# A three-layer field-interaction kernel: V and A as streaming matrix products, A reordered through a DRAM scratch, five replicas of X, one mixed 128-row tile

## The reference

```
Xi = X0                                    # [b, 32, d]
for W, b in ((W1, b1), (W2, b2), (W3, b3)):
    Wr = W.reshape(128, 32, m)             # m = fields of Xi: 32, then 128, 128
    Xi = einsum('bhd,bmd,ohm->bod', X0, Xi, Wr) + b[None, :, None]
    pools.append(Xi.sum(axis=-1))
y = concat(pools) @ fc_W.T + fc_b          # [64, 1]
```

## Time and profile before

| what | value |
|---|---|
| median of 3 runs | 107.69 us (107.32 to 108.24) |
| the profiled execution | 108.17 us, its span 106.4 us |
| around the span in the profiled execution | 1.77 us |
| PE busy | 81.1 us of the span |
| DVE, ACT, POOL busy | 62.7, 34.8, 38.5 us |
| moved by DMA | 15.64 MB |

### The profile page before, as it was taken

The page is one execution under the profiler, slowest core; times in us unless marked ns, Lnnn a source line. Parts: engine busy times, 40 slices in busy tenths (PEclk is TensorE's granted clock), DMA queues, the critical chain, the costliest instruction groups (busy, mean ns, idle before and its releaser), DMA issues.

```text
span 106.4 us, 960 instructions
## 1 busy us (share of the span) xinstructions
PE 81.1 (76%) x303; PEld 60.8 (57%) x303; DVE 62.7 (59%) x87; ACT 34.8 (33%) x66; POOL 38.5 (36%) x31
## 2 busy tenths in 40 slices
PE   0042692006999999934999999999999999999921
PEld 0031570004899879934767766776677666866710
DVE  0239999998600029959995999829987011020072
ACT  4008400019500277462809722076190200201100
POOL 2033099930700079955602309245062204022000
PEclk9999999755555555555589999999999999999998
DMA  3959999920599998971074643700000000000000
GB/s 94 402 135 353 419 431 419 434 117 0 112 110 125 393 404 250 116 310 65 0 219 176 194 200 89 305 3 0 0 6 0 0 0 0 0 0 0 0 0 0
DMA packets 3464, 15.64 MB, mean 147 GB/s; under 512 B 516, under 2 KB 644, under 8 KB 2180
## 3 DMA queue, kind: packets, MB, share of 16 engines
q1 hardware_dynamic: 3460, 15.59, 45.0%
HBM read 14.27 MB, written 0.00 MB: 134 GB/s over the span
## 4 chain that ended last, share of the span: by engine, by line
PE 69%; DVE 16%; DMA 5%; ACT 4%; issue 3%; SPq 0%; DVEq 0%
PE x_ps L538 27%; PE a_ps L538 27%; PE a_ps L599 11%; DMA rep<-xr 5%; DVE w_sb L180 5%; DVE v L476 2%; DVE z_ps L406 2%; ACT feat L313 2%; DVE feat L415 2%; DVE rows_sb L437 1%; PE a_ps L526 1%; ACT v_all L313 1%; ACT a_sb L313 1%; DVE total L509 1%; DVE total L506 1%
## 5 line engine op out<-in xcount | busy, mean ns | idle before, releaser
L538 PE MATMUL x_ps<-feat,w_hi 128*128 128x512 f32 x64 | 27.9, 495 | 2.4 <-DMA fc_all<-fc 2.4
L406 DVE TENSOR_TENSOR z_ps<-rep 128x512 f32<-128x512 f32 x24 | 21.2, 910 | 13.2 <-DMA rep<-xr 12.3
L538 PE MATMUL a_ps<-feat,a_hi 128*128 128x512 f32 x64 | 21.9, 403 | 0.0
L251 POOL TENSOR_TENSOR z_pool<-rep 128x512 f32<-128x512 f32 x8 | 14.9, 1858 | 15.3 <-DMA rep<-xr 13.6
L538 PEld LDWEIGHTS x_ps<-feat,w_hi 128*128 128x128 f32 x64 | 15.1, 236 | 7.0 <-DMA fc_all<-fc 2.8
L313 ACT ACTIVATE feat<-z_ps 128x512 fp32r<-128x512 f32 x24 | 13.9, 592 | 14.1 <-DVE z_ps L406 14.1
L285 POOL TENSOR_TENSOR x<-x 128x512 f32<-128x512 f32 x6 | 8.5, 1413 | 23.5 <-DVE x L466 23.5
L466 DVE SCALAR_TENSOR_TENSOR x<-a_ps,vec,x 128x512 f32<-128x512 f32 x8 | 6.0, 744 | 18.5 <-PE a_ps L538 18.5
L538 PE MATMUL x_ps<-feat,w_lo 128*128 128x512 f32 x32 | 15.6, 488 | 1.6 <-DVE w_tail L456 1.6
L415 DVE TENSOR_TENSOR feat<-z_ps,feat 128x512 fp32r<-128x512 f32 x24 | 16.0, 682 | 1.0 <-ACT feat L313 0.8
L599 PEld LDWEIGHTS a_ps<-v_all,w_sb 128*128 128x128 f32 x60 | 14.6, 331 | 1.6 <-issue 0.9
(11 more groups left out here) (66 smaller groups left out, 69.0 us busy)
## 6 DMA issues: line engine op xcount, KB each, us to landing
rep<-xr SPq DMA_DIRECT2D x8, 1024.0 KB, 5.4
w_sb<-w SPq DMA_DIRECT2D x4, 512.0 KB, 8.8
w_sb<-w SPq DMA_DIRECT2D x2, 1024.0 KB, 13.5
w_sb<-w SPq DMA_DIRECT2D x1, 560.0 KB, 3.8
tail<-z_hi SPq DMA_DIRECT2D x2, 256.0 KB, 5.4
xp<-x SPq DMA_DIRECT2D x1, 512.0 KB, 8.1
lin<-xp_lo SPq DMA_DIRECT2D x1, 512.0 KB, 6.7
xa<-x SPq DMA_DIRECT2D x1, 256.0 KB, 6.9
```

The source lines that it names most:

```text
L251: nc.gpsimd.tensor_tensor(z_pool[:, c % 2, :], rep[:, c % 2, left, :], rep[:, c % 2, right, :], ALU.mult).then_inc(zp_done, 1)
L406: nc.vector.tensor_tensor(z_ps[:, k, :], rep[:, c % 2, left, :], rep[:, c % 2, right, :], ALU.mult).then_inc(z_done, 1)
L538: last = nc.tensor.matmul(bank, w, f, **kw)
```

## The change

- V is a product on PE: `window` is zero but for the column of fc, and 32 matmuls (128 x 32 stationary, 128 columns of W3 streaming in f32) put the 32 fields of V on 32 rows in four column groups. One transpose brings it back. W3 is loaded in its own order, in pieces of 1 KB.
- A is 8 f32 matmuls with V stationary (64 columns) and 512 columns of W2 streaming. ACT saves them (`save_a`), six DMAs store them in a DRAM scratch `a_dram`, and eleven DMAs load them back in feature order, each pair in both orders, in pieces of 512 bytes. No transpose of A is left. DVE adds the two orders (`make_a`) inside chunk 3.
- W1 comes from the host in feature order, so its transposes go too.
- `rep` has five replicas instead of four, in two DMAs. The first holds the left fields of all pairs.
- The tail, and X in high and low parts, are one tile of 128 rows (`mixed`), filled by four DMAs of 16 rows and two of 32 rows from SBUF to SBUF. `lin_hi` goes.
- The order of PE, ACT and DVE is written out anew; the first reduction over d stands ahead of the last product.

```diff
-J = P // H
+J = 4
+REPS = TILES + 1
+X_HI, X_LO, Z_HI, Z_LO, Z_HI2, Z_PAD = 0, 32, 64, 80, 96, 112
+A_ROWS, A_COLS = 64, H + HALF
+ROW = A_COLS * M
+ROUNDS = 4
+    a_dram = nc.dram_tensor("a_dram", (A_ROWS, A_COLS * M), f32, kind="Internal").ap()
-        tail = sb("tail", [3 * HALF, CHUNKS, N], f32r)
-        lin = sb("lin", [3 * H, CHUNKS, N], f32r)
-        rep = sb("rep", [P, 2, 4, N])
+        mixed = sb("mixed", [P, CHUNKS, N], f32r)
+        rep = sb("rep", [P, 2, REPS, N])
...
 # sync
-                    sp.wait_ge(lin_hi_done, c - 1)
-                sp.dma_start(rep[:, c % 2, :, :], xr[c]).then_inc(rep_in[c % 2], 16)
+                sp.dma_start(rep[:, c % 2, 0:2, :], xr[c, :, 0:2, :]).then_inc(rep_in[c % 2][0], 16)
+                sp.dma_start(rep[:, c % 2, 2:, :], xr[c, :, 2:, :]).then_inc(rep_in[c % 2][1], 16)
+            def store_a(g, t, col):
+                to = bass.AP(a_dram.tensor, col * M, [[ROW, A_ROWS], [8 * M, 2], [1, N]])
+                sp.dma_start(to, at_sb[64 * g:64 * g + 64, t:t + 2, :]).then_inc(a_out, 16)
+            def load_f(to, offset, dims):
+                sp.dma_start(to, bass.AP(a_dram.tensor, offset, dims + [[1, M]])).then_inc(f_in, 16)
...
+            for t in range(ROUNDS):
+                part = slice(t * 8 * M, (t + 1) * 8 * M)
+                sp.dma_start(w2_sb[:, part], w2[:, part]).then_inc(w2_in[t], 16)
+            sp.dma_start(xp[:, :, :].rearrange("p d b -> p (d b)"),
+                         x.rearrange("h (c n) -> (h c) n", c=4)).then_inc(xp_in, 16)
+            for row, part, done in ((Z_HI, z16_hi, hi16_done), (Z_HI2, z16_hi, hi16_done),
+                                    (Z_PAD, z16_hi, hi16_done), (Z_LO, z16_lo, lo16_done)):
                 sp.wait_ge(done, 1)
+                sp.dma_start(mixed[row:row + HALF, :, :].bitcast(f32), part[:, :].bitcast(f32)).then_inc(z16_in, 16)
             load_replicas(2)
+            for row, part, done in ((X_HI, xp_hi, xp_hi_done), (X_LO, xp_lo, xp_lo_done)):
+                sp.wait_ge(done, 1)
+                sp.dma_start(mixed[row:row + H, :, :]..., part[:, :]...).then_inc(x_lin_in, 16)
             load_replicas(3)
-            sp.wait_ge(xp_lo_done, 1)
-            sp.dma_start(lin[2 * H:3 * H, :, :]..., xp_lo[:, :]...).then_inc(lin_lo_in, 16)
+            sp.wait_ge(a_saved, 2)
+            for g in range(2):
+                store_a(g, 0, 4 * g)
+                store_a(g, 0, H + 4 * g)
+            sp.wait_ge(a_saved, 4)
+            for g in range(2):
+                store_a(g, 2, HALF + 4 * g)
+            sp.wait_ge(zeros_done, 5)
+            sp.wait_ge(a_out, A_OUT)
+            for k in range(TILES):
+                load_f(f1[:, k, :], 4 * k * ROW, [[ROW + M, H], [ROW, J]])
+                load_f(f2[:, k, :], 4 * k * M, [[ROW + M, H], [M, J]])
+            load_f(f1[Z_HI:Z_PAD, TILES, :], HALF * ROW, [[0, 3], [ROW + M, HALF]])
+            load_f(f2[Z_HI:Z_PAD, TILES, :], HALF * M, [[0, 3], [ROW + M, HALF]])
+            load_f(f1[0:Z_HI, TILES, :], FC2_ROW * ROW, [[0, 2], [M, H]])
             for c in range(4, CHUNKS):
                 load_replicas(c)
...
 # scalar: hi(1, 3), xp_hi, q_sb, save_a(0), hi(2, 0), save_a(1), hi(2, 1), save_a(2), hi(2, 2),
 #   save_a(3), hi(2, 3), save_x1(0), save_x1(1), hi(3, 0..3), save_x1(2), a_hi, hi(4, 0..3), ...
+            def save_a(t):
+                act.wait_ge(a_ready, t + 1)
+                copy(at_sb[:, t, :], round_ps[t][:, :]).then_inc(a_saved, 1)
...
 # vector
+            def make_a():
+                dve.wait_ge(f_in, F_IN)
+                both_orders(f1, f2, f_sum)
+            for c in range(1, CHUNKS):
+                mult(c, 0)
+                mult(c, 1)
+                lo(c, 0)
+                mult(c, 2)
+                lo(c, 1)
+                if c == 3:
+                    make_a()
+                lo(c, 2)
+                lo(c, 3)
+                if c == 3:
+                    a_low()
+                if c >= 5:
+                    product(c - 5)
+            for c in range(3, CHUNKS - 1):
+                product(c)
             dve.wait_ge(acc_done, CHUNKS - 2)
             nc.vector.tensor_reduce(total[:, 0, :], ...)
+            product(CHUNKS - 1)
             dve.wait_ge(prod_done, CHUNKS)
             nc.vector.tensor_reduce(total[:, 1, :], ...)
...
 # tensor
+            x1_main(0)
+            pe.wait_ge(window_done, 1)
+            for i in range(8):
+                if i % 2 == 0:
+                    pe.wait_ge(w3_in[i // 2], 16)
+                for g in range(4):
+                    last = nc.tensor.matmul(vt_ps[32 * g:32 * g + 32, :], window[:, H - 1 - i:2 * H - 1 - i],
+                                            w3_sb[:, 8 * g + i, :], start=(i == 0), stop=(i == 7))
+            nc.tensor.transpose(v_ps, vt_sb[:, :], ident[:, :]).then_inc(v_ready, 1)
+            x1_main(1)
+            for t in range(ROUNDS):
+                pe.wait_ge(w2_in[t], 16)
+                for g in range(2):
+                    first = (8 * t + 4 * g) * M
+                    last = nc.tensor.matmul(round_ps[t][64 * g:64 * g + 64, :], v_st[:, :],
+                                            w2_sb[:, first:first + N], start=True, stop=True)
+                last.then_inc(a_ready, 1)
+            x1_tail(0)      # x1_tail(c): one matmul on `mixed`; waits for z16_in, from c = 2 on for x_lin_in
+            x1_tail(1)
             x1_product(2)
+            x1_product(3)
+            pe.wait_ge(a_hi_done, 1)
+            pe.wait_ge(a_lo_done, 3)
+            a_product(0)    # 12 matmuls and two of 128 rows on `mixed`
+            a_product(1)
+            for c in range(2, CHUNKS - 2):
+                x1_product(c + 2)
+                a_product(c)
+            a_product(CHUNKS - 2)
+            a_product(CHUNKS - 1)
```

More of the change, by code:

```diff
@@ new lines, in _ @@
+            hi(1, 3)
+            act.wait_ge(xp_in, 16)
+            copy(xp_hi[:, :], xp[:, :, :].rearrange("p d b -> p (d b)")).then_inc(xp_hi_done, 1)
+            act.wait_ge(q_ready, 1)
+            copy(q_sb[:, :], q_ps).then_inc(q_saved, 1)
+            save_a(0)
+            hi(2, 0)
+            save_a(1)
+            hi(2, 1)
+            save_a(2)
+            hi(2, 2)
+            save_a(3)
+            hi(2, 3)
+            act.wait_ge(vec_in, 32)
+            save_x1(0)
+            save_x1(1)
@@ L397, in _, with mult @@
+            for k in range(TILES):
+                hi(3, k)
+            save_x1(2)
+            act.wait_ge(f_sum, 2)
+            copy(a_hi[:, :, :], f1[:, :, :]).then_inc(a_hi_done, 1)
+            for k in range(TILES):
+                hi(4, k)
+            save_x1(3)
+            for c in range(5, CHUNKS):
+                for k in range(TILES):
+                    hi(c, k)
+                save_x1(c - 1)
+            save_x1(CHUNKS - 1)
         @block.vector
         def _(dve):
-            def pairs(n):
-                c, k = divmod(n, DVE_TILES)
-                left, right = PAIR[k]
-                dve.wait_ge(rep_in[c % 2], 16 * (c // 2 + 1))
+            def mult(c, k):
+                dve.wait_ge(rep_in[c % 2][0], 16 * (c // 2 + 1))
+                if k > 0:
+                    dve.wait_ge(rep_in[c % 2][1], 16 * (c // 2 + 1))
@@ L463, in product, with a_low @@
+            def a_low():
+                dve.wait_ge(f_sum, 2)
+                dve.wait_ge(a_hi_done, 1)
+                nc.vector.tensor_tensor(c_lo[0:H, :], f1[0:H, TILES, :], a_hi[0:H, TILES, :].bitcast(f32),
+                                        ALU.subtract).then_inc(a_lo_done, 1)
+                weights_lo(f1, a_hi, a_lo, a_lo_done)
             def product(c):
@@ L490, in _ @@
[L490 to L503 removed]
+            dve.wait_ge(not_diag_done, 2)
@@ L532, in terms, with main_terms @@
-            def terms(bank, c, w_hi, w_lo, w_tail, linear, between=()):
-                between = list(between)
-                placed = [0]
-                def mm(w, f, **kw):
-                    last = nc.tensor.matmul(bank, w, f, **kw)
-                    placed[0] += 1
-                    for _ in range(2):
-                        if between and placed[0] > FIRST_BETWEEN:
-                            between.pop(0)()
-                    return last
+            def main_terms(bank, c, high, low):
@@ L551, in terms @@
                     pe.wait_ge(lo_done, TILES * c + k + 1)
[L552 to L563 removed]
+                    nc.tensor.matmul(bank, high[:, k, :], feat[:, c, 1, k, :], start=False, stop=False)
@@ L564, in x1_product, with x1_main, x1_tail @@
+            def x1_main(c):
                 if c >= 2:
                     pe.wait_ge(x1_saved, c - 1)
-                last = terms(x1_ps[c % 2][:, :], c, w1_hi, w1_lo, w1_tail, False, between)
-                if c:
-                    last.then_inc(x1_ready, 1)
-            def x1_tail_of_chunk_0():
-                pe.wait_ge(tail_in, 48)
-                nc.tensor.matmul(x1_ps[0][:, :], w1_tail[:, :], tail[:, 0, :],
```

(11 more changed lines are left out.)

551 lines of the change are left out of this document (201 added, 350 removed).

## The result

Median of 4 runs: 116.1 us (115.38 to 117.54), against 107.97 us (107.32 to 108.32) for the kernel before. The ratio is 1.074, with a 95% interval of 1.065 to 1.083: slower by 8.1 us. The profiled execution took 115.38 us, its span 113.7 us; the forecast was 114.1 and 112.3.

A forecast was written before the change was run, and what follows sets the result against it. PE was taken as the bound after T, with T set by the DMA queue: 69.1 + 43.2 = 112.3 us of span, with 1.77 around it 114.1 profiled, hence a median of 113.6 us; range 106 to 122 us.

The forecast's parts named there:

- steps 1 to 3: DMA queue up to replica 3: the 16-row and 32-row copies take 19.0 us instead of 12.0; replica 3 at 49.7.
- Rival (d): Narrow copies don't hold up what stands behind them; stores start at about 44, 105.2 us in all; chance 0.14.
- Rival (a): X copies go at twice the row's rate, replica 3 and all behind 4.75 us sooner: 108.8 us; chance 0.09.
- step 5: Stores of A to DRAM: 7.2 us, between bounds of 3.7 and 14.3; landed at 57.9 us.
- Rival (b): Reading SBUF is what is slow in the copies; stores take 14.3 us, 120.7 us in all; chance 0.18.
- step 6: SP's eleven loads of A: 5.0 us of issue and 2.9 of landing, the last in at 65.8 us.
- rival (c): A's round trip is cheap: stores 3.7 us, issues 0.33 each, short landing; 107.8 us, no change; chance 0.14.
- step 7: make_a on DVE in the middle of chunk 3, with the work that waits for it: 3.3 us, to 69.1 us.
- T: The moment PE can start the a products, forecast at 69.1 us.
- Behind T: PE's a and x1 products 37.4 us, small y products 0.4, cold start 1.5, end 3.9: 43.2 us.
- step 4: PE's V and A at up to 13.7 us each, hidden by the queue by 1 us at worst, more than 6 at best.
- the prediction's own signs of being wrong: Stores leave before replica 3 has landed, take less than 4 us or more than 14, or PE isn't the bound after T.

The follow-up runs named there:

- e1: The changed kernel with its six SBUF-to-SBUF copies going to 128 partitions of spare tiles, tail pairs and linear terms left out of the result: 102.46 us, ratio 0.954.
- e7: The changed kernel with the mixed tile's parts stored wide to DRAM and loaded back in one load of 128 rows: 108.37 us, ratio 1.013.
- e4: The changed kernel with the x1 tail matmul on 64 rows of the mixed tile for all chunks: 118.22 us, ratio 1.103.
- e9: The changed kernel with each of the eight matmuls for A issued twice: 117.36 us (114.39 to 120.33).
- e10: e8 with SP waiting for ScalarE's loads of A before it issues replica 4: 105.49 us, ratio 0.986.
- e8: e7 with five of A's eleven loads on ScalarE, all of A saved before chunk 2, and product(c - 4) instead of product(c - 5): 112.03 us, ratio 1.049.
- e12: e8 with all A loads on SP, A's stores before the mixed tile's load, replica 3 after A's loads, A made before chunk 3: 105.70 us, ratio 0.984.

## Why the prediction was right, step by step

The forecast was a median of 113.6 us; it was 116.1. Of the profiled execution, which was the fastest of the four, 115.38 for 114.1. The sum is right in kind; by its steps:

- **The queue behind the narrow copies** (steps 1 to 3) was the main term, and it held. The 16-row copies ended at 35 us (34.1 forecast) and the 32-row copies at 47 (46.6). e1 shows the cause by taking the width away. Replica 2 was off in part: its first half came at 37.20 as forecast, but the second half at 41.28, mixed with the X copies. ScalarE's last save of A stood behind it (44.19), and so did the last store's issue (44.80). That cost nothing here, since the queue was full of the X copies until 47 and of replica 3 behind them.
- **Rival (d)**, faster because the copies hold nothing up, had a point of truth: the window 38 to 47 has 150 GB/s, not 110. From 25 to 47 us 3.73 MB moved, and the six copies and replica 2 are 3.41, so some 0.3 MB of what stood behind them (replica 3 or the stores) went beside them. It was far from letting A through.
- **Rival (a)**, the X copies at twice the rate, falls: 1.05 MB from about 37.7 to 47 us is 113 GB/s, and all that moved in the window 38 to 47 is 150.
- **The stores** (step 5) were priced at 7.2 us between 3.7 and 14.3; they landed at 55.19, not 57.9. From 47 to 53.6 us 2.43 MB went at 368 GB/s. Less replica 3 that leaves 1.1 MB of stores, at nearly the load rate. So the low bound was right. Rival (b) is refuted: reading SBUF from 64 or 128 partitions is not slow (402 GB/s in e7).
- **The loads of A** (step 6) were the term that was sized too low: 5.0 us of issue and 2.9 of landing against 7.31 and 2.4. I took 0.45 us an issue from rows that had 0.43 to 0.65, and they took 0.66. That gave back 1.8 of the 2.7 us won at the stores; so rival (c), the cheap round trip, held in its first half and failed in its second.
- **`make_a` and the end of `x1_product(3)`** (step 7): 3.9 us from A in to `a_product(0)`, not 3.3. DVE was done in 3.3, but PE had the five matmuls of `x1_product(3)` at the low clock. T came to 68.83 against 69.1, by errors that cancel.
- **Behind T** 43.2 us were forecast and 44.9 measured. The prices of the products were right (0.225 us a matmul, and e4 gives the steps back). The cold start cost 0.7 and not 1.5: the starts are 0.43 us apart only until 70.1. The end took 4.1 and not 3.9, and some longer steps between matmuls, such as 0.39 us at 86.39, make up the rest. What failed is the sentence that `a_product(2)` meets no stall. DVE's `product(0)` ended at 80.3 us, T + 11.5, where T + 10.7 was forecast (the low part just ahead of it took 1.62 us instead of some 0.7), and PE was ready at T + 10.2 and not at T + 10.9, since the cold start had cost less. So PE stood 1.38 us. I had called it close and then given it no price in the sum.
- **PE's new work** (step 4) was priced at up to 27.4 us and called hidden. Hidden it was, but the price was wrong: V took 1.95 us and A 4.1. The step's cover of 1 us at the worst was in truth over 11 us for the last round of A (its matmuls end at 32.6, its save starts at 44.19).

That T came out within 0.3 us is luck: the stores were 2.7 us cheaper than forecast and the loads 1.8 dearer. And A's landing in DRAM differs by up to 4.8 us among kernels with the same DMA order up to there (55.19 here, 59.94 in e9).

Two of the prediction's own signs of being wrong came close. The stores took about 4 us of moving (1.57 MB at 368 to 406 GB/s is 4.3 to 3.9). And a first part of them may have left before replica 3 had landed (51.40), in the 0.3 MB above.

## What to carry to other kernels

A copy from SBUF to 16 or 32 partitions ran here at about 110 GB/s, where one to 128 partitions ran at about 400, and every transfer issued behind it pays: look for a DMA share near 1.0 beside a low GB/s, and gather the parts wide in DRAM instead. When a chain of transfers sets the time, their order in the queues counts more than any engine's work, big loads wanted later are better held until small ones on another queue, wanted now, have landed, and an added wait can be a gain (e10). After each cut look again at what the first wait in every engine's program is: twice here (e8 and e12) something that the chain needed stood behind `save_x1(2)` in ScalarE's order.

## What the runs showed of the hardware that was not expected

- f32 matmuls that use different column groups of TensorE overlap: V's 64 passes took 1.95 us, 0.03 us each at the full clock, where a pass of 128 columns alone took 0.21 at the low clock, so some 0.11 at the full one (an estimate, at half the time). A's sixteen records of 512 columns, two groups, took 4.1 us, 0.26 each, where four times 0.11 would be 0.44.
- A change of the number of rows between matmuls adds 0.4 us to the starts around a single narrow tile (0.32, 0.42, 0.34 against 0.23), with 48 rows as with 64. In e4 this did not lengthen the part behind T (45.0 us against 44.9), as a wait there went away.
- A DMA issue on SP with pieces of 512 bytes takes 0.66 us (7.31 for eleven), the plain replica loads from 62 us on 0.33 to 0.43 in the same trace.
- Small loads issued before or beside large ones on another queue can land after them: in e8 replica 4 was in by 59.85 us and A at 63.60; in e10, with one wait added, A was in at 56.31.
- 32 rows from DRAM: about 200 GB/s; 32 rows from SBUF: 110; copies and loads of 128 rows together: 402 and 406 (e7, e1).
- Behind narrow copies the rest of the queue came at times that differ by 5 us from kernel to kernel (replica 2 at 37.20 to 42.56 us, against 30.00 to 31.05 without them).
